# Summed-value and attention projections as three passes of split parts instead of full f32, with the weights split in the stream and at its end

## The chip, the cores and the metric

One core of one Trainium2 chip. The metric is the device time of one execution in microseconds (us), the median of several runs. Engines are TensorE (PE; its weight loads are PEld), VectorE (DVE), ScalarE (ACT), GpSimd (POOL) and SyncE (SP), which issues nearly all loads.

## The reference

One perceiver-like block on x (256 x 512) with a context of 25,088 rows of 512:

```python
x = x + xattn(layernorm(x), ctx)     # sigmoid(q k^T / sqrt(128)) @ (ctx Wv^T + bv), no softmax
x = x + attn(layernorm(x))           # 16 heads of 32, latent k/v of 128, rotary part of 32, causal
x = x + ffn(layernorm(x))            # top-1 of 8 experts: relu(g)^2 * u, masked by the one-hot, @ wd
```

In the cross attention q = Wq x + bq and k = Wk ctx + bk. All is float32.

## The kernel before

**Split operands.** A large product of two f32 matrices is made from three matmuls of float32r operands: each operand is split into a high part (a ScalarE copy to float32r) and a low part (a VectorE subtraction), and high x high, high x low and low x high add up in PSUM. The context, the sigmoid weights, the keys and the expert weights go this way. Other products are full f32 matmuls, each of which the profile shows as two records.

**The stream.** The context comes in 49 blocks of 512 rows, once transposed (`rawt`) and once as it is (`rawn`). For block b the loop at L364 queues scores(b), weights(b) (sigmoid, split), keys(b+1), the splits of the blocks ahead, and values(b), which adds sigmoid^T ctx for both halves of 128 queries into banks 4 and 5. Wv is not applied per context row: it is applied once to the sum. One spare load goes out per block: first the list `late` (L349: wv, latent and rotary weights, gate, tables, bv), then in odd blocks from 15 the expert weights: `up_load` (L354) brings half a megabyte into the staging tile `wst`, and `up_split` (L358) splits it two blocks later. Each tensor of `ups` (L351) has one load and one split; there are eight. At blocks NB-3 and NB-2 come the loads of wq, wo (`DWO`, L387) and the first two parts of wd, into places that the stream has left.

**The end of the stream.** The last blocks are written out by hand (L390 to L402) so that the first half (r = 0) of the sum is done before the second. Then, for a half r: `sum_out` (L422) copies the sum to `y_s`, which is `h_s`; four transposes; `sum_turned` (L425) evicts them on ScalarE to `yT`, which is `hT`; `project_v` (L428) multiplies by wv in full f32: 4 matmuls of 128x512. The bias part, bv times the row sums of the sigmoid, is added to x by two VectorE operations (L466). `norm_stats` (L437) adds the projection to x and computes the statistics, with the square root on ScalarE (L442), and `norm_rows` (L444) normalizes. The second half's values matmuls (L469) lie between the two projections. `latents` (L492) and `query` (L536) follow.

**The attention.** Six units of heads are pipelined by hand (from L676): scores, maxima, exponentials (ScalarE), transposes on TensorE, evictions of them (`a_evac`, L613, on the engine that is named), the product with v (`a_pv`, L621). `a_sums` (L635) makes reciprocals of the sums and spreads them per head (`eexp`), `a_spread` (L642) turns them on TensorE, `a_spread_out` (L649) evicts them to `rr`, and `a_norm` (L652) multiplies the result of a half by them into `aT`. `project_o` (L658) multiplies by wo in full f32, 4 matmuls of 128x512 into bank 1. Then come the residual add, the normalization, and the experts (`experts_up` L761, `down` L793), whose input is split by `norm_parts` (L738). wd is split there by `down_part` (L807).

Each engine executes its queue in the order of the `put` calls, and waits on a semaphore ahead of an instruction where a mark is listed:

```python
XM = [project_v(0, 2, [YT[0], LATE, ZF[last]])]                      # L463
DONE.append(values(last, (1, 2, 3), (1,), sig="av1"))                # L469
X1[0], RS[0] = norm_stats(0, 2, [XM[0], XB])                         # L471
XM.append(project_v(1, 3, [YT[1]]))                                  # L481
XO = [project_o(0, 1, [])]                                           # L720
X2[0], RS[0] = norm_stats(0, 1, [XO[0]])                             # L725
XO.append(project_o(1, 1, [X2[0]]))                                  # L823
```

Of the kernel before, what the change touches and what calls it, by code (L numbers as in the profile page):

```python
# [13 lines left out]
P = 128  # L14
# [44 lines left out]
def program(nc, x, ctxn, ctxt, wkt, wqt, wvt, bqk, bv, kvd, kup, vup, wq, qrope, krope, wo, gate, wg, wu, wd,  # L59
# [3 lines left out]
    with ExitStack() as ctx:  # L63
# [3 lines left out]
        def sb(name, shape, dt=F32):  # L67
            return ctx.enter_context(nc.sbuf_tensor(name, shape, dt))

        ps = [ctx.enter_context(nc.psum_tensor(f"ps{i}", [P, 1024], F32)) for i in range(4)]  # L70

# [6 lines left out]
        x_s = sb("x_s", [P, 2, D])  # L78
        h_s = sb("h_s", [P, 2, D])
        hT = sb("hT", [P, 4, T])  # L80
        st = sb("st", [P, 64])
        sq = sb("sq", [1, 8])
        zacc = sb("zacc", [P, 1024])
        zcol = sb("zcol", [P, 2])
        zsum = sb("zsum", [P, T])
        wz = sb("wz", [P, 512], BF16)
        one_s = sb("one_s", [P, 1])
        wv_s = sb("wv_s", [P, 4, D])
        bv_s = sb("bv_s", [P, D])
# [40 lines left out]
        zl = [sm(f"zl{i}", [P, 1024], F32R) for i in range(2)]  # L130
        wst = sm("wst", [P, 1024])
        stream.close()
# [5 lines left out]
        hTl = sb("hTl", [P, 4, T], F32R)  # L138
        wo_s = sb("wo_s", [P, 4, D])
        wds = [sb(f"wds{i}", [P, 1024]) for i in range(2)]  # L140
        aT = sb("aT", [P, 4, T])
        eexp = sb("eexp", [P, 16, 32])
        rr = sb("rr", [P, D])
        wdh = sb("wdh", [P, 8, D], F32R)
# [11 lines left out]
        ka = sa("ka", [P, 8, T])  # L156
        w_s = [sa(f"w{i}", [P, 512]) for i in range(4)]
        rtx = ExitStack()
# [51 lines left out]
        def split_n(b, k, later=False):  # L210
# [11 lines left out]
            return low if later else low()  # L222

        WZ = put("gpsimd", lambda e: e.memset(wz[:], 0.0), (), "wz")
        for k in range(14):
# [120 lines left out]
        for k in range(2):  # L346
            split_t(1, k)()

        late = [(wv_s[:], wvt), (kvd_s[:], kvd), (qr_s[:], qrope), (kr_s[:], krope), (kup_s[:], kup),  # L349
                (vup_s[:], vup), (gate_s[:], gate), (cs_s[:], cossin), (mk_s[:], mask), (io_s[:], iota), (bv_s[:], bv)]  # L350
        ups = [(w, h, l, c) for w, h, l in ((wg, wgh, wgl), (wu, wuh, wul)) for c in range(4)]  # L351
        UP, DUP = [], []

        def up_load(i):  # L354
            w, h, l, c = ups[i]
            DUP.append(dma("sync", wst[:], w[:, c].rearrange("p a b -> p (a b)"), "dup", UP[-1:]))

        def up_split(i):  # L358
            w, h, l, c = ups[i]
            hi, lo = (t[:, c].rearrange("p a b -> p (a b)") for t in (h, l))  # L360
            m = put("scalar", lambda e: e.activation(hi, wst[:], ACT.Copy), DUP[-1:], "uph")
            UP.append(put("vector", lambda e: e.tensor_tensor(lo, wst[:], hi, ALU.subtract), [m], "upl"))

# [42 lines left out]
        def half(r):  # L406
            return slice(r * P, r * P + P)
# [17 lines left out]
        def sum_turned(r, bk, mark):  # L425
            return put("scalar", lambda e: e.activation(yT[:, :, half(r)], chunks(bk), ACT.Copy), [mark], "yt_e")

        def project_v(r, bk, wait):  # L428
            for c in range(4):
                m = put("tensor", lambda e, c=c: e.matmul(bank(bk), yT[:, c, half(r)], wv_s[:, c, :], start=(c == 0),  # L430
                                                          stop=(c == 3)), wait, "xp" if c == 3 else None)
            return m

        def col(r, k, n=1):
# [25 lines left out]
        for r in range(2):  # L460
            m = put("tensor", lambda e, r=r: e.matmul(bank(0)[:, r:r + 1], zsum[:, half(r)], one_s[:],
                                                      start=True, stop=True), [ZS, ONE, KPL[last]], "zs1" if r else None)
        XM = [project_v(0, 2, [YT[0], LATE, ZF[last]])]  # L463
        ZR = put("vector", lambda e: e.tensor_copy(zcol[:], bank(0)[:, 0:2]), [m], "zr")
        for r in range(2):
            XB = put("vector", lambda e, r=r: e.scalar_tensor_tensor(  # L466
                out=x_s[:, r, :], in0=bv_s[:], scalar=zcol[:, r:r + 1], in1=x_s[:, r, :], op0=ALU.mult, op1=ALU.add),
                [ZR, LATE], "xb")
        DONE.append(values(last, (1, 2, 3), (1,), sig="av1"))  # L469
        X1, RS = [None, None], [None, None]  # L470
# [9 lines left out]
        HT = [put("vector", lambda e: e.tensor_scalar(hT[:, :, half(0)], chunks(0), 2.0, None, ALU.mult), [n], "lne_v")]  # L480
        XM.append(project_v(1, 3, [YT[1]]))  # L481

# [9 lines left out]
        def latents(r, b_c, b_q, b_k, b_v, wait):  # L492
            n = half(r)
            m = project(bank(b_c)[:, 0:P], lambda c: kvd_s[:, c, :], n, [HT[r], *wait], "ck")
            CKV[r] = put("scalar", lambda e: e.activation(ckv[:, n], bank(b_c)[:, 0:P], ACT.Copy), [m], "ckv")
            QR[r] = project(bank(b_q)[:, 0:P], lambda c: qr_s[:, c, :], n, [X1[r], YT[1]], "qr")
            KR[r] = put("tensor", lambda e: e.matmul(bank(b_c)[:, 0:P], kr_s[:], ckv[:, n], start=True, stop=True),
                        [CKV[r]], "kr")
            for t in range(4):
                KT[r] = put("tensor", lambda e, t=t: e.matmul(bank(b_k)[:, P * t:P * t + P], kup_s[:, P * t:P * t + P],  # L500
                                                              ckv[:, n], start=(t == 0), stop=(t == 3)), [X1[r]],
                            "k" if t == 3 else None)
            VT[r] = put("tensor", lambda e: e.matmul(bank(b_v), ckv[:, n], vup_s[:], start=True, stop=True), [], "v")
# [131 lines left out]
        def a_sums(qt):  # L635
            m = put("vector", lambda e: e.reciprocal(einv[:, qt, :], esum[:, qt, :]),
                    [EX[p, u] for p in range(NU) if units[p][0] == qt for u in range(2)], "rc")
            return put("vector", lambda e: e.tensor_copy(
                eexp[:], einv[:, qt, :].rearrange("p (h o) -> p h o", o=1).to_broadcast([P, 16, 32])),
                [m] + ([RR[0]] if qt else []), "rc")  # L640
# [8 lines left out]
        def a_spread_out(qt, bk, mark):  # L649
            RR[qt] = put("scalar", lambda e: e.activation(rr[:], bank(bk), ACT.Copy), [mark] + ([AE[0]] if qt else []), "rr_s")  # L650

        def a_norm(qt):  # L652
            AE[qt] = put("vector", lambda e: e.tensor_tensor(
                aT[:, :, half(qt)], bank(1 + qt).rearrange("p (t n) -> p t n", t=4),
                rr[:].rearrange("p (t n) -> p t n", t=4), ALU.mult),
                [RR[qt]] + [PV[p] for p in range(NU) if units[p][0] == qt], "ae")

        def project_o(r, bk, wait):  # L658
            for t in range(4):
                m = put("tensor", lambda e, t=t: e.matmul(bank(bk), aT[:, t, half(r)], wo_s[:, t, :], start=(t == 0),  # L660
                                                          stop=(t == 3)), [AE[r], DWO, *wait], "wo" if t == 3 else None)
            return m
# [48 lines left out]
        a_scores(5)  # L711
        a_norm(0)
        maxima(5)
        turns(4)
        a_evac(4, 0, "scalar")
        a_evac(4, 1, "vector")
        exps(5)
        a_pv(3)
        table(ACT.Sqrt)
        XO = [project_o(0, 1, [])]  # L720
        X2 = [None, None]
        f = a_spread(1, 4, [a_sums(1), EX[4, 0]])
        a_spread_out(1, 4, f)
        turns(5)
        X2[0], RS[0] = norm_stats(0, 1, [XO[0]])  # L725
        a_evac(5, 0, "scalar")
# [3 lines left out]
        a_pv(5)  # L730
        a_norm(1)

# [28 lines left out]
        def experts_up(r, k, j, wait):  # L761
            wh, wl = ((wgh, wgl), (wuh, wul))[j]
            n = 0
            for c in range(4):
                for w, h in ((wh, hTh), (wh, hTl), (wl, hTh)):
                    n += 1
                    GU[r, k, j] = put("tensor", lambda e, w=w, h=h, c=c, n=n: e.matmul(  # L767
                        bank(UB[k][j]), h[:, c, half(r)], w[:, c, 4 * k:4 * k + 4, :].rearrange("p a b -> p (a b)"),
                        start=(n == 1), stop=(n == 12)), [HP[r][0], UP[-1], *wait], "gu" if n == 12 else None)
# [37 lines left out]
        def down_part(k):  # L807
            n = slice(2 * k, 2 * k + 2)
            h_, l_ = (t[:, n].rearrange("p a b -> p (a b)") for t in (wdh, wdl))
            m = put("scalar", lambda e: e.activation(h_, wds[k % 2][:], ACT.Copy), [DWD[k], DONE[1]], "wdh")  # L810
            WDP.append(put("vector", lambda e: e.tensor_tensor(l_, wds[k % 2][:], h_, ALU.subtract), [m], "wdl"))
# [9 lines left out]

        m = norm_turn(0, 6, [EX[4, 1]])
        XO.append(project_o(1, 1, [X2[0]]))  # L823
        norm_parts(0, 6, m)
# [123 lines left out]
```

How the kernel before makes its waits and increments, by code:

```python
    def play(self, eng, e):  # L49
        for item in self.lists[eng]:
            if item[0] == "wait":
                e.wait_ge(item[1], item[2])
            else:
                ins = item[1](e)
                if item[2] is not None:
                    ins.then_inc(item[2], item[3])
```

## Time and profile before

| | |
|---|---|
| median of 3 runs | 585.0 us (584.59 to 585.08) |
| profiled execution | 584.42 us, span 582.6 us |
| busy: PE, DVE, ACT | 571.4, 448.5, 392.8 us |
| chain that ended last | PE 93%, DVE 3%, ACT 2% |
| granted clock of TensorE | 1.0 |

The span reaches from the first to the last instruction in the profile; the rest of the execution's time lies around it. Busy times overlap between engines. The chain is followed back from the last instruction, at each step to what released it, or to the one before it on its engine.

### The profile page before, as it was taken

What the parts mean: (1) busy time and instruction counts of PE and PEld (TensorE: products, weight loads), DVE (VectorE), ACT (ScalarE), POOL (GpSimd) and SP (SyncE); (2) the same over time, 40 slices, a digit from 0 to 9 for tenths busy, and PEclk for the clock granted to TensorE, in tenths of its full rate; (3) what the DMA queues carried; (4) which work ended last, traced back from release to release, by engine and by line L of the source; (5) the groups of instructions that cost most, each with busy time, mean ns of one, the idle gap of its engine ahead of it and who ended that gap; (6) DMA issues with size and microseconds to landing.
All of it is one profiled execution on the core that took longest, in us unless ns stands there. A gap on an engine that the chain in (4) does not pass through costs nothing.

```text
span 582.6 us, 7921 instructions
## 1 busy us (share of the span) xinstructions
PE 571.4 (98%) x2966; PEld 472.8 (81%) x2966; DVE 448.5 (77%) x499; ACT 392.8 (67%) x529; POOL 1.7 (0%) x7
## 2 busy tenths in 40 slices
PE   7899999999999999999999999999999999999998
PEld 4788888888888888888888888888888885766787
DVE  5887878787878798889788978787878775786642
ACT  5776677776767787868786767777776772586321
POOL 1000000000000000000000000000000000000000
DMA  8678877777777877787778676767676752000200
GB/s 278 206 242 271 257 245 243 221 224 224 228 229 243 260 246 233 244 258 251 240 237 259 216 228 208 231 210 228 208 244 193 246 174 118 1 2 2 72 1 36
DMA packets 33094, 115.87 MB, mean 199 GB/s; under 512 B 4065, under 2 KB 4769, under 8 KB 32673
## 3 DMA queue, kind: packets, MB, share of 16 engines
q1 hardware_dynamic: 32480, 114.79, 62.4%
q10 hardware_dynamic: 576, 0.59, 0.3%
q8 instruction: 23, 0.38, 0.3%
q14 instruction: 15, 0.11, 0.1%
HBM read 114.84 MB, written 0.52 MB: 198 GB/s over the span
## 4 chain that ended last, share of the span: by engine, by line
PE 93%; DVE 3%; ACT 2%; DMA 1%; issue 1%; DVEq 0%; SPq 0%
PE ps L327 45%; PE ps L275 22%; PE ps L292 12%; PE ps L767 4%; PE ps L799 2%; PE ps L486 2%; PE ps L660 1%; PE ps L430 1%; ACT w L601 1%; DMA rawt<-in_ctxt 1%; PE ps L579 1%; DMA x_s<-in_x 1%; PE ps L608 1%; DVE zl L307 0%; DVE tl L204 0%
## 5 line engine op out<-in xcount | busy, mean ns | idle before, releaser
L327 PE MATMUL ps<-nh,zl 128*128 128x512 f32 x392 | 144.8, 390 | 0.4 <-DVE zl L307 0.3
L327 PE MATMUL ps<-nh,zh 128*128 128x512 f32 x392 | 144.9, 390 | 0.0
L327 PE MATMUL ps<-nl,zh 128*128 128x512 f32 x392 | 144.4, 389 | 0.0
L307 DVE TENSOR_TENSOR zl<-zf,zh 128x1024 fp32r<-128x1024 f32 x49 | 60.1, 1226 | 83.4 <-ACT zh L306 83.4
L216 DVE TENSOR_TENSOR nl<-rawn,nh 128x1024 fp32r<-128x1024 f32 x98 | 116.7, 1221 | 4.2 <-ACT nh L213 2.5
L204 DVE TENSOR_TENSOR tl<-rawt,th 128x1024 fp32r<-128x1024 f32 x98 | 115.6, 1218 | 2.2 <-ACT th L199 2.1
L213 ACT ACTIVATE nh<-rawn 128x1024 fp32r<-128x1024 f32 x98 | 101.6, 1056 | 14.1 <-DMA rawn<-in_ctxn 13.5
L199 ACT ACTIVATE th<-rawt 128x1024 fp32r<-128x1024 f32 x98 | 98.6, 1053 | 5.4 <-DMA rawt<-in_ctxt 5.4
L302 ACT ACTIVATE zf<-ps 128x512 f32<-128x512 f32 x98 | 58.2, 597 | 56.7 <-PE ps L292 51.1
L327 PEld LDWEIGHTS ps<-nh,zl 128*128 128x128 f32 x392 | 73.4, 188 | 17.0 <-DVE zl L307 1.7
L327 PEld LDWEIGHTS ps<-nh,zh 128*128 128x128 f32 x392 | 73.4, 188 | 15.6 <-issue 0.2
L327 PEld LDWEIGHTS ps<-nl,zh 128*128 128x128 f32 x392 | 73.6, 188 | 15.3
L280 ACT ACTIVATE kph<-ps,bqk_s 128x512 fp32r<-128x512 f32 x49 | 33.8, 689 | 49.4 <-PE ps L275 49.4
L310 DVE TENSOR_TENSOR zacc<-zacc,zf 128x1024 f32<-128x1024 f32 x49 | 59.8, 1221 | 0.0
L292 PE MATMUL ps<-qph,kph 128*128 128x256 f32 x196 | 55.3, 282 | 1.2 <-DVE qpl L343 1.2
L292 PE MATMUL ps<-qph,kpl 128*128 128x256 f32 x196 | 55.5, 283 | 0.0
L292 PE MATMUL ps<-qpl,kph 128*128 128x256 f32 x196 | 55.4, 283 | 0.0
L275 PE MATMUL ps<-th,wkh 128*128 128x512 f32 x196 | 54.1, 396 | 0.7 <-ACT th L199 0.7
L306 ACT ACTIVATE zh<-zf 128x1024 fp32r<-128x1024 f32 x49 | 52.1, 1063 | 1.6
L275 PE MATMUL ps<-th,wkl 128*128 128x512 f32 x196 | 52.6, 390 | 0.0
L275 PE MATMUL ps<-tl,wkh 128*128 128x512 f32 x196 | 52.4, 389 | 0.0
L275 PEld LDWEIGHTS ps<-th,wkl 128*128 128x128 f32 x196 | 36.8, 188 | 8.3
(154 smaller groups left out, 575.0 us busy)
## 6 DMA issues: line engine op xcount, KB each, us to landing
rawt<-in_ctxt SPq DMA_DIRECT2D x98, 512.0 KB, 4.7
rawn<-in_ctxn SPq DMA_DIRECT2D x98, 512.0 KB, 6.4
wst<-in_wg SPq DMA_DIRECT2D x4, 512.0 KB, 7.3
wst<-in_wu SPq DMA_DIRECT2D x4, 512.0 KB, 7.4
wds<-in_wd SPq DMA_DIRECT2D x4, 512.0 KB, 4.8
wv_s<-in_wvt SPq DMA_DIRECT2D x1, 1024.0 KB, 9.9
wq_s<-in_wq SPq DMA_DIRECT2D x1, 1024.0 KB, 7.1
wo_s<-in_wo SPq DMA_DIRECT2D x1, 1024.0 KB, 4.7
```

Source lines behind the costliest of these rows:

```text
L199: Th[b, k] = put("scalar", lambda e: e.activation(th[:, n], rawt[:, n], ACT.Copy), [t_ld[b, k]] + before, "th")
L204: Tl[b, k] = put("vector", lambda e: e.tensor_tensor(tl[:, n], rawt[:, n], th[:, n], ALU.subtract), [t_ld[b, k], Th[b, k]], "tl")
L213: Nh[b, k] = put("scalar", lambda e: e.activation(nh[s_][:, n], rawn[:, n], ACT.Copy), [n_ld[b, k]] + av, "nh")
L216: Nl[b, k] = put("vector", lambda e: e.tensor_tensor(nl[s_][:, n], rawn[:, n], nh[s_][:, n], ALU.subtract), [n_ld[b, k], Nh[b, k]] + av, "nl")
L275: KP[b] = put("tensor", lambda e, w=w, t=t, c=c, i=i: e.matmul(bank(b % 2), w[:, c * P:(c + 1) * P], t[:, c * 512:(c + 1) * 512], start=(i ...
L280: KPH[b] = put("scalar", lambda e: e.activation(kph[:], bank(b % 2), ACT.Identity, bias=bqk_s[:, 1:2]), [KP[b], DBK] + ([S[b - 1]] if b el ...
L292: m = put("tensor", lambda e, o=o, js=js, k=k, w=w, i=i: e.matmul(o, k[:, js], w[:], start=(i == 0), stop=(i == 2)), wait, "s" if (i == 2 ...
L302: m = put("scalar", lambda e, g=g, gs=gs: e.activation(zf[:, gs], bank(2 + g), ACT.Sigmoid, scale=SC), [S[b, g]] + ([ZL[b - 1], ZA[b - 1]] ...
L306: ZH[b] = put("scalar", lambda e: e.activation(zh[b % 2][:], zf[:], ACT.Copy), [ZF[b]] + av, "zh")
L307: ZL[b] = put("vector", lambda e: e.tensor_tensor(zl[b % 2][:], zf[:], zh[b % 2][:], ALU.subtract), [ZH[b]] + av, "zl")
L310: ZA[b] = put("vector", lambda e: e.tensor_tensor(zacc[:], zacc[:], zf[:], ALU.add), [ZF[b], Z0] + ([ZA[b - 1]] if b else []), "za")
L327: AV[b] = put("tensor", lambda e, z=z, n=n, i=i, j=j, r=r: e.matmul(bank(4 + r), z[:, j * T + r * P:j * T + r * P + P], n[:, j * D:(j + 1) ...
```

## The change

`project_v` and `project_o` become three passes of float32r parts, 12 matmuls for 4. Each needs its two operands in high and low parts:

- wv leaves `late`. It is loaded in two pieces as the first two entries of `ups`, now ten, and split like the expert weights. The staging tile is `h_s`.
- wo is split by `split_o` in two pieces, the high ones on ScalarE right after the first `project_v` is queued, the low ones on VectorE ahead of the first residual add and after the first `hT` eviction.
- `sum_turned` evicts the high part on ScalarE and the low part on VectorE.
- `a_norm` makes the high part first; the returned function makes the full product and the low part. For the first half it is queued after the last `turns(4)` and its first eviction.
- the first `project_o` goes to bank 6, and the second norm's waits follow.
- the three passes of `experts_up` are reordered, and wd's split waits for the second `project_o`.
- tiles share places: yTh with hT, yTl with eexp, rr and zacc, w_s with wvh, aT and the parts of a with wvl, wol with wo_s, wst with h_s.

```diff
-        late = [(wv_s[:], wvt), (kvd_s[:], kvd), (qr_s[:], qrope), ...
+        late = [(kvd_s[:], kvd), (qr_s[:], qrope), ...
+        ups = [tuple(flat(t[:, 2 * k:2 * k + 2]) for t in (wvt, wvh, wvl)) for k in range(2)]
+        ups += [tuple(flat(t[:, c]) for t in m) for m in ((wg, wgh, wgl), (wu, wuh, wul)) for c in range(4)]
...
         def up_load(i):
-            w, h, l, c = ups[i]
-            DUP.append(dma("sync", wst[:], w[:, c].rearrange("p a b -> p (a b)"), "dup", UP[-1:]))
+            DUP.append(dma("sync", wst, ups[i][0], "dup", UP[-1:]))
...
         def sum_turned(r, bk, mark):
-            return put("scalar", lambda e: e.activation(yT[:, :, half(r)], chunks(bk), ACT.Copy), [mark], "yt_e")
+            hi = put("scalar", lambda e: e.activation(yTh[:, :, half(r)], chunks(bk), ACT.Copy), [mark], "yt_e")
+            lo = put("vector", lambda e: e.tensor_tensor(yTl[:, :, half(r)], chunks(bk), yTh[:, :, half(r)], ALU.subtract),
+                     [hi, ZS], "yt_l")
+            return hi, lo
...
         def project_v(r, bk, wait):
-            for c in range(4):
-                m = put("tensor", lambda e, c=c: e.matmul(bank(bk), yT[:, c, half(r)], wv_s[:, c, :], start=(c == 0),
-                                                          stop=(c == 3)), wait, "xp" if c == 3 else None)
+            hi, lo = YT[r]
+            for i, (t, w, mark) in enumerate(((yTh, wvh, hi), (yTh, wvl, hi), (yTl, wvh, lo))):
+                for c in range(4):
+                    m = put("tensor", lambda e, t=t, w=w, c=c, i=i: e.matmul(
+                        bank(bk), t[:, c, half(r)], w[:, c, :], start=(i == 0 and c == 0), stop=(i == 2 and c == 3)),
+                        [mark, UP[1], *wait], "xp" if (i, c) == (2, 3) else None)
             return m
+
+        def split_o(k):
+            n = slice(2 * k, 2 * k + 2)
+            hi = put("scalar", lambda e: e.activation(flat(woh[:, n]), flat(wo_s[:, n]), ACT.Copy), [DWO], "woh")
+            return lambda: put("vector", lambda e: e.tensor_tensor(flat(wol[:, n]), flat(wo_s[:, n]), flat(woh[:, n]),
+                                                                   ALU.subtract), [hi], "wol")
...
-        XM = [project_v(0, 2, [YT[0], LATE, ZF[last]])]
+        XM = [project_v(0, 2, [ZF[last]])]
+        low_o = [split_o(k) for k in range(2)]
         ZR = put("vector", lambda e: e.tensor_copy(zcol[:], bank(0)[:, 0:2]), [m], "zr")
...
+        low_o[0]()
         DONE.append(values(last, (1, 2, 3), (1,), sig="av1"))
...
         HT = [put("vector", lambda e: e.tensor_scalar(hT[:, :, half(0)], chunks(0), 2.0, None, ALU.mult), [n], "lne_v")]
-        XM.append(project_v(1, 3, [YT[1]]))
+        WOL = low_o[1]()
+        XM.append(project_v(1, 3, []))
...
         def a_norm(qt):
...
+            AH[qt] = put("vector", lambda e: e.tensor_tensor(aTh[:, :, n], src, r4, ALU.mult), done, "ah")
+
+            def rest():
+                AE[qt] = put("vector", lambda e: e.tensor_tensor(aT[:, :, n], src, r4, ALU.mult), [], "ae")
+                AL[qt] = put("vector", lambda e: e.tensor_tensor(aTl[:, :, n], aT[:, :, n], aTh[:, :, n], ALU.subtract),
+                             [AE[qt]], "al")
+
+            return rest
 
         def project_o(r, bk, wait):
...
+            for i, (t, w, mark) in enumerate(((aTh, woh, AH[r]), (aTh, wol, AH[r]), (aTl, woh, AL[r]))):
+                for c in range(4):
+                    m = put("tensor", lambda e, t=t, w=w, c=c, i=i: e.matmul(
+                        bank(bk), t[:, c, n], w[:, c, :], start=(i == 0 and c == 0), stop=(i == 2 and c == 3)),
+                        [mark, WOL, *wait],
+                        "wo" if (i, c) == (2, 3) else None)
...
-        a_norm(0)
+        low_a = a_norm(0)
         maxima(5)
         turns(4)
         a_evac(4, 0, "scalar")
+        low_a()
         a_evac(4, 1, "vector")
         exps(5)
         a_pv(3)
         table(ACT.Sqrt)
-        XO = [project_o(0, 1, [])]
+        XO = [project_o(0, 6, [EX[4, 1]])]
...
-        X2[0], RS[0] = norm_stats(0, 1, [XO[0]])
+        X2[0], RS[0] = norm_stats(0, 6, [XO[0]])
...
-        a_norm(1)
+        a_norm(1)()
...
-                for w, h in ((wh, hTh), (wh, hTl), (wl, hTh)):
+                for w, h in ((wh, hTh), (wl, hTh), (wh, hTl)):
...
-            m = put("scalar", lambda e: e.activation(h_, wds[k % 2][:], ACT.Copy), [DWD[k], DONE[1]], "wdh")
+            m = put("scalar", lambda e: e.activation(h_, wds[k % 2][:], ACT.Copy), [DWD[k], XO[1]], "wdh")
...
-        m = norm_turn(0, 6, [EX[4, 1]])
-        XO.append(project_o(1, 1, [X2[0]]))
+        m = norm_turn(0, 6, [X2[0]])
+        XO.append(project_o(1, 1, [AE[0]]))
```

## Rows read from the trace of the kernel before

**Rows 1.** The page: the span, and busy time of each engine

```profile
span 582.6 us, 7921 instructions
...
PE 571.4 (98%) x2966; PEld 472.8 (81%) x2966; DVE 448.5 (77%) x499; ACT 392.8 (67%) x529; POOL 1.7 (0%) x7
```

**Rows 2.** Chain of waits, 180 to 220 us: start, duration, engine, tile, line

```profile
184.97 5.44 PE ps L327 x24
190.41 1.43 PE ps L292 x12
191.84 2.75 PE ps L275 x12
```

**Rows 3.** Windows of two blocks: length, busy (instructions) per engine, PE clock, DMA

```profile
240.00:259.20 19.20, 19.20 (x97) 16.38 (x96) 15.94 (x16) 14.74 (x17) 0.00 (x0) 1.00 0.82 245
...
343.20:362.40 19.20, 19.20 (x97) 16.34 (x97) 15.08 (x15) 13.63 (x17) 0.00 (x0) 1.00 0.73 219
```

**Rows 4.** Chain of waits, 480 to 545 us, around the summed values

```profile
485.28 3.56 PE ps L430 x8
488.86 0.70 DVE x_s L438
...
492.86 3.59 PE ps L430 x8
```

**Rows 5.** Chain of waits, 490 us to the end

```profile
530.39 3.65 PE ps L660 x8
...
534.06 0.70 DVE x_s L438
...
538.79 3.70 PE ps L660 x8
542.49 5.61 PE ps L767 x24
...
574.30 5.76 PE ps L799 x48
```

**Rows 6.** The page's costly groups: busy, mean ns of one, idle before

```profile
L327 PE MATMUL ps<-nh,zh 128*128 128x512 f32 x392 | 144.9, 390 | 0.0
```

**Rows 7.** Tiles wst and wkl: ns min/median/max, first and last start

```profile
L361 ACT ACTIVATE wuh<-wst x4: 1043/1044/1047, 266.8 to 324.1; 128x1024 fp32r<-128x1024 f32 x4
L362 DVE TENSOR_TENSOR wul<-wst,wuh x4: 1221/1223/1224, 268.4 to 326.1; 128x1024 fp32r<-128x1024 f32 x4
...
L256 DVE TENSOR_TENSOR wkl<-wk_s,wkh x1: 682/682/682, 8.4 to 8.4; 128x512 fp32r<-128x512 f32 x1
```

**Rows 8.** Timeline of ScalarE, 480 to 496 us

```profile
484.28 0.60 ACT L426 ACTIVATE hT<-ps 128x512 f32<-128x512 f32 x1 [0.74 <-PE ps L411]
490.71 0.20 ACT L442 ACTIVATE st<-st 128x1 f32<-128x1 f32 x1 [5.84 <-DVE st L441]
490.92 0.66 ACT L472 ACTIVATE h_s<-ps 128x256 f32<-128x256 f32 x2
```

**Rows 9.** Timeline of VectorE, 484 to 496 us

```profile
485.31 0.16 DVE L464 COPY zcol<-ps 128x2 f32<-128x2 f32 x1 [1.45 <-PE ps L461]
485.51 1.41 DVE L466 SCALAR_TENSOR_TENSOR x_s<-bv_s,zcol,x_s 128x512 f32<-128x512 f32 x2
```

**Rows 10.** Tiles wo_s and wv_s: issue of the load and its landing

```profile
L47 SPq DMA_DIRECT2D wo_s<-in_wo x1: 328/328/328, 478.2 to 478.2; - x1
...
DMA to landing us min/median/max: 4.7/4.7/4.7
...
DMA to landing us min/median/max: 9.9/9.9/9.9
```

**Rows 11.** Timeline of VectorE, 518 to 536 us

```profile
530.63 0.68 DVE L619 COPY wT<-ps 128x512 f32<-128x512 f32 x1
532.02 0.25 DVE L636 RECIPROCAL einv<-esum 128x16 f32<-128x16 f32 x1 [0.71 <-ACT w L601]
532.31 0.43 DVE L638 COPY eexp<-einv 128x512 f32<-128x512 f32 x1
```

More of the change, by code:

```diff
@@ L68, in sb, with several, once @@
             return ctx.enter_context(nc.sbuf_tensor(name, shape, dt))
+        def several(name, n, shape, dt=F32):
+            with ExitStack() as group:
+                return [group.enter_context(nc.sbuf_tensor(f"{name}{i}", shape, dt)) for i in range(n)]
+        def once(name, shape, dt=F32):
+            with nc.sbuf_tensor(name, shape, dt) as t:
+                return t
         ps = [ctx.enter_context(nc.psum_tensor(f"ps{i}", [P, 1024], F32)) for i in range(4)]
@@ L79, in program @@
         h_s = sb("h_s", [P, 2, D])
+        yTh = once("yTh", [P, 4, T], F32R)
         hT = sb("hT", [P, 4, T])
@@ L82, in program @@
         sq = sb("sq", [1, 8])
+        yTl = once("yTl", [P, 4, T], F32R)
+        eexp, rr = (t[:] for t in several("er", 2, [P, D]))
+        eexp = eexp.rearrange("p (h o) -> p h o", o=32)
         zacc = sb("zacc", [P, 1024])
         zcol = sb("zcol", [P, 2])
+        wz = once("wz", [P, 512], BF16)
         zsum = sb("zsum", [P, T])
-        wz = sb("wz", [P, 512], BF16)
         one_s = sb("one_s", [P, 1])
-        wv_s = sb("wv_s", [P, 4, D])
+        w_s = several("w", 4, [P, 512])
+        wvh = sb("wvh", [P, 4, D], F32R)
+        aT, _ = several("aT", 2, [P, 4, T])
+        aTl, aTh = several("aTs", 2, [P, 4, T], F32R)
+        wvl = sb("wvl", [P, 4, D], F32R)
         bv_s = sb("bv_s", [P, D])
@@ L130, in program @@
         zl = [sm(f"zl{i}", [P, 1024], F32R) for i in range(2)]
-        wst = sm("wst", [P, 1024])
         stream.close()
@@ L138, in program @@
         hTl = sb("hTl", [P, 4, T], F32R)
-        wo_s = sb("wo_s", [P, 4, D])
+        wo_s = once("wo_s", [P, 4, D])
+        wol = sb("wol", [P, 4, D], F32R)
+        woh = sb("woh", [P, 4, D], F32R)
         wds = [sb(f"wds{i}", [P, 1024]) for i in range(2)]
-        aT = sb("aT", [P, 4, T])
-        eexp = sb("eexp", [P, 16, 32])
-        rr = sb("rr", [P, D])
         wdh = sb("wdh", [P, 8, D], F32R)
@@ L156, in program @@
         ka = sa("ka", [P, 8, T])
-        w_s = [sa(f"w{i}", [P, 512]) for i in range(4)]
         rtx = ExitStack()
@@ L222, in split_n @@
             return low if later else low()
+        wst = h_s[:].rearrange("p a b -> p (a b)")
         WZ = put("gpsimd", lambda e: e.memset(wz[:], 0.0), (), "wz")
@@ L347, in program, with flat @@
             split_t(1, k)()
-        late = [(wv_s[:], wvt), (kvd_s[:], kvd), (qr_s[:], qrope), (kr_s[:], krope), (kup_s[:], kup),
+        late = [(kvd_s[:], kvd), (qr_s[:], qrope), (kr_s[:], krope), (kup_s[:], kup),
                 (vup_s[:], vup), (gate_s[:], gate), (cs_s[:], cossin), (mk_s[:], mask), (io_s[:], iota), (bv_s[:], bv)]
-        ups = [(w, h, l, c) for w, h, l in ((wg, wgh, wgl), (wu, wuh, wul)) for c in range(4)]
+        def flat(t):
+            return t.rearrange("p a b -> p (a b)")
+        ups = [tuple(flat(t[:, 2 * k:2 * k + 2]) for t in (wvt, wvh, wvl)) for k in range(2)]
+        ups += [tuple(flat(t[:, c]) for t in m) for m in ((wg, wgh, wgl), (wu, wuh, wul)) for c in range(4)]
         UP, DUP = [], []
         def up_load(i):
-            w, h, l, c = ups[i]
-            DUP.append(dma("sync", wst[:], w[:, c].rearrange("p a b -> p (a b)"), "dup", UP[-1:]))
+            DUP.append(dma("sync", wst, ups[i][0], "dup", UP[-1:]))
         def up_split(i):
[L359 to L362, printed above, removed]
+            _, hi, lo = ups[i]
+            m = put("scalar", lambda e: e.activation(hi, wst, ACT.Copy), DUP[-1:], "uph")
+            UP.append(put("vector", lambda e: e.tensor_tensor(lo, wst, hi, ALU.subtract), [m], "upl"))
         for b in range(NB):
@@ L495, in latents @@
             CKV[r] = put("scalar", lambda e: e.activation(ckv[:, n], bank(b_c)[:, 0:P], ACT.Copy), [m], "ckv")
-            QR[r] = project(bank(b_q)[:, 0:P], lambda c: qr_s[:, c, :], n, [X1[r], YT[1]], "qr")
+            QR[r] = project(bank(b_q)[:, 0:P], lambda c: qr_s[:, c, :], n, [X1[r], YT[1][0]], "qr")
             KR[r] = put("tensor", lambda e: e.matmul(bank(b_c)[:, 0:P], kr_s[:], ckv[:, n], start=True, stop=True),
@@ L638, in a_sums @@
             return put("vector", lambda e: e.tensor_copy(
-                eexp[:], einv[:, qt, :].rearrange("p (h o) -> p h o", o=1).to_broadcast([P, 16, 32])),
+                eexp, einv[:, qt, :].rearrange("p (h o) -> p h o", o=1).to_broadcast([P, 16, 32])),
                 [m] + ([RR[0]] if qt else []), "rc")
@@ L649, in a_spread_out @@
         def a_spread_out(qt, bk, mark):
-            RR[qt] = put("scalar", lambda e: e.activation(rr[:], bank(bk), ACT.Copy), [mark] + ([AE[0]] if qt else []), "rr_s")
+            RR[qt] = put("scalar", lambda e: e.activation(rr, bank(bk), ACT.Copy), [mark] + ([AE[0]] if qt else []), "rr_s")
+        AH, AL = {}, {}
         def a_norm(qt):
[L653 to L656, printed above, removed]
-        def project_o(r, bk, wait):
-            for t in range(4):
-                m = put("tensor", lambda e, t=t: e.matmul(bank(bk), aT[:, t, half(r)], wo_s[:, t, :], start=(t == 0),
-                                                          stop=(t == 3)), [AE[r], DWO, *wait], "wo" if t == 3 else None)
+            src = bank(1 + qt).rearrange("p (t n) -> p t n", t=4)
+            r4 = rr[:].rearrange("p (t n) -> p t n", t=4)
+            n = half(qt)
+            done = [RR[qt]] + [PV[p] for p in range(NU) if units[p][0] == qt]
+            AH[qt] = put("vector", lambda e: e.tensor_tensor(aTh[:, :, n], src, r4, ALU.mult), done, "ah")
[4 more added lines that the diff above has]
+            return rest
+        def project_o(r, bk, wait):
+            n = half(r)
+            for i, (t, w, mark) in enumerate(((aTh, woh, AH[r]), (aTh, wol, AH[r]), (aTl, woh, AL[r]))):
[4 more added lines that the diff above has]
+                        "wo" if (i, c) == (2, 3) else None)
             return m
```

## Prediction

> **What bounds the kernel now.** I read the page first. TensorE (PE) is busy 571 of 582.6 us [rows 1], so only what shortens its queue, or a wait of that queue, can move the end. The chain of waits in a stretch of the stream shows the period of one block of context: values 5.44, scores 1.43, key projection 2.75, that is 9.62 us of TensorE back to back, with nobody else in it [rows 2]. The windows say how much room the others have there: in 19.2 us TensorE is busy 19.20, VectorE 15.94 and ScalarE 14.74 where two expert weights are split, 15.08 and 13.63 where none is, with the same 97 matmuls, and the granted clock is 1.00, the higher level of 2.4 GHz [rows 3]. So the stream is TensorE's alone. After it, from about 480 us, the chain goes back and forth: each projection that the change touches stands on it (3.56 and 3.59 us for the summed values, 3.65 and 3.70 us for the attention), followed by VectorE's residual add and statistics [rows 4, 5]. From 542.49 us TensorE is on the chain without a break to 580.05 [rows 5], so whatever is gained up to the fourth projection should reach the end whole.
>
> **Price of a projection.** Before: four full f32 matmuls, 8 records, 3.56 to 3.70 us [rows 4, 5]. After: 12 matmuls of reduced-precision operands, same 128x512 size. Their nearest row is the expert matmuls in the same part of the kernel, 24 in 5.61 us, 0.234 each [rows 5]; in the stream 24 take 5.44, 0.227 each [rows 2]. One such record lasts 0.39 against a spacing of 0.234 [rows 6], so a last one adds 0.16 for whoever waits for it. 12 x 0.234 + 0.16 = 2.97 us against 3.56, 3.59 and 3.65: a gain of 0.59, 0.62 and 0.68. I take 0.64 for each of the four. The lower bound is 0.59. For the upper one, suppose that a reduced-precision pass takes no longer than a quarter of a full f32 matmul: (3.65 - 0.16) / 16 = 0.218, so 12 x 0.218 + 0.16 = 2.78, and a gain of 0.87.
>
> The rows put the gain at 0.64, since the 12 passes are spaced 0.234 apart and the quarter of a full f32 matmul is only 0.218. The Trainium skill has one spacing for both: "FP8 and Floating Point Precision", section TensorE Precision Notes, counts full f32 as four passes through the array, and "TensorE: Matmul & The Clock Gate", section Back-to-back issue gap, gives a pass N/2.4 + 2.5 ns, about 216 ns for 512 columns; 16 against 12 such passes would save 0.86. The trace agrees for full f32 and not for the reduced operands, and the measured spacing decides; equal spacing is a rival below.
>
> **Splits in the stream.** wv (1 MB) is no longer one late load but two staged ones, so the queue of expert weights has ten entries for eight: two more ScalarE copies of 1.04 and VectorE subtractions of 1.22 us [rows 7], in blocks of their own. They are covered by VectorE's 3.3 us and ScalarE's 4.5 us of room in two blocks [rows 3]; uncovered they would cost 2.3 each. The bytes on SP's queue are the same, and each staged load waits for a split that is already done in the blocks that do this now, where TensorE doesn't stop. Cost 0. The staging buffer now shares its place with h_s, idle in the stream: 0.
>
> **First projection of the summed values.** The high part replaces an eviction of the same size, 484.28 to 484.88 [rows 8]. The low part is new on VectorE: 0.69 (an operation from PSUM, as the residual add in [rows 4]), to 485.61; TensorE needs it after 8 of 12 matmuls, near 487.0, so it costs nothing there. But it stands ahead of the copy of the row sums and of the two bias additions (0.16 and 1.41 us [rows 9]), which end near 487.3, and behind these the change puts the first half of wo's low part, 1.22 [rows 7], to 488.5. TensorE is done with the projection at 488.83 - 0.64 = 488.2. So the residual add starts at 488.5, not 488.2, where it was at 488.86 [rows 4]: **0.34** of the 0.64 arrive. wo's two high parts (2 x 1.04) fill a ScalarE that waits 5.8 us there [rows 8]; they need wo_s, issued at 478.2 and landed 4.7 us later, at 482.9 [rows 10], two us early.
>
> The 0.34 go on: statistics, square root at 490.37, then the evictions of the second half's sum, which stand behind that root on ScalarE at 490.92 [rows 8], then transposes. The values matmuls they also need end earlier by 0.64.
>
> **Second projection of the summed values.** Its low part follows the row normalization on VectorE and is ready 0.7 after its high part, against 1.87 us (8 matmuls) of cover. hT's eviction and wo's second low part (1.22) come next and end near 495.0; the residual add waits for TensorE until 495.5. All covered: **0.64**. The latents and the attention up to 530 us are bound to this end on both engines, so everything there moves by 0.98.
>
> **First attention projection** (times as before, without that 0.98). The high part takes the place of aT's multiply. The full product and the low part stand between the last maxima and the copy of a transposed tile that ran at 530.63 [rows 11]. They cost 0.69 + 0.68 (the second is the one subtraction of this size within SBUF, [rows 7]) with two handovers: 1.4. The copy then ends at 532.7, the reciprocal and its spread (from 532.02 to 532.74 before [rows 11]) at 533.5. TensorE starts the projection at 530.39 as before, runs 8 matmuls to 532.26, when the low part (ready near 532.05) is just there, and ends at 530.39 + 2.97 = 533.4. So the residual add moves from 534.06 [rows 5] to about 533.55: **0.50**, bounds 0.3 and 0.64. Moving it to bank 6 costs nothing: that score tile has been read by then. The exponentials on ScalarE don't wait for the added work.
>
> **Second attention projection.** The chain comes through the last evictions and the product with v ahead of it, all 0.50 earlier, to the high part. The full and low products end 1.45 after it, against 1.87 of cover, and the next stage's low part (0.69) behind them still ends some 0.9 before the experts need it. **0.64**. The swapped order of the expert passes changes no count: all of them wait for the low part anyway. The later wait of wd's split costs 0: ScalarE reaches it after the square root, which comes after that projection.
>
> Sum: 0.34 + 0.64 + 0.50 + 0.64 = 2.12. The profiled execution took 584.42 us (span 582.6 and 1.8 around it), 0.6 under the median of 585.0; 584.42 - 2.12 = 582.3, and against the median **582.9 us**.
>
> **Rivals.**
> - *VectorE's queue eats more.* Both first halves end in VectorE, not in TensorE, by 0.3 and 0.1. If its added pieces with their handovers take 0.35 to 0.5 longer in each place, the first halves bring nothing and 2 x 0.64 = 1.3 is left: 583.7. For it: the order of its queue. Against: all pieces have rows.
> - *TensorE gives the full four.* If VectorE overlaps its operations a little more, 4 x 0.64 = 2.56: 582.4.
> - *Equal spacing.* If the new passes run at the 0.218 of full f32, 0.87 comes in each of the two that TensorE alone bounds and 0.84 together where VectorE bounds: 2.58, 582.4; with VectorE out of the way too, 4 x 0.87 = 3.5, 581.5. The spacings of [rows 2, 5] speak against it. This is the Trainium skill's rule named above.
> - *No gain.* The latents' stage or attention is bound by something that doesn't move with the projections (a queue on ScalarE, say). Then at most the last 0.64 to 1.1 stay: 584 to 584.4. The chain shows no such wait in the places that I followed.
> - *Slower: wo_s is late.* wo's high part stands on ScalarE and its low part on VectorE ahead of the residual add. If the load lands at L, that add cannot start before L + 1.06 + 1.26. At 488.2 or later, 10.0 us after issue instead of 4.7, the whole gain of 2.1 is gone, and from 11.2 us on the kernel is slower by over 1.2: 586.2 and more. For it: the other 1 MB load, wv_s, took 9.9 in the full stream [rows 10]. Against: this one runs when the stream's loads are over.
> - *The passes are no cheaper*, because the split operands are treated as full f32: 12 at 0.86 would be 10 us each. The key projections of the stream, split in the same way, exclude it.
>
> **How the numbers follow.** Forecast 0.67; VectorE's queue 0.13; full four 0.07; equal spacing 0.04; no gain 0.04; wo_s late 0.04; passes no cheaper, or what I haven't seen, 0.01. A measurement of this kernel can tell about 0.2%, 1.2 us, from no change, that is 583.8. Faster takes the forecast, the two larger gains and 0.08 of VectorE's case: 0.86. Same takes the rest of that case and no gain: 0.09. Slower: 0.05. The range runs from 581.6, nearly the whole of equal spacing, to 584.0, just past the case of VectorE's queue.
>
> **What would show it.** In the changed profile: the block period still 9.62; each projection 12 matmuls at about 0.234; the first residual add released by wo's low part on VectorE and not by TensorE, 0.3 earlier than now; TensorE's first latents 1.0 earlier; at the first attention projection the residual add 1.5 earlier; the experts 2.1 earlier (from 542.49 to 540.4) and from there the same 37.6 us. It is wrong if the period grows, if TensorE idles over 0.2 us between the eighth and the ninth matmul of a projection, or if the stretch from 496.5 to 530.4 gets longer.

## The result and the profile after

The change makes the kernel faster, by 0.4%: 582.60 us median of 7 runs (581.88 to 583.38) against 584.52 (584.30 to 585.08) in the same comparison, ratio 0.9964, 95% interval 0.9952 to 0.9975. Two later comparisons of the same kernel gave 582.08 against 584.68 (0.9957, 0.9945 to 0.9969) and 581.97 against 584.63 (0.9958, 0.9945 to 0.9972). Over all 18 runs of it the median is 582.2, some 2.4 us under before. The forecast was 2.1, from 585.0 to 582.9.

The profiled execution took 581.88 us, 2.54 less than the one of before. Its page, span and busy times (compare [rows 1]):

```profile
span 580.1 us, 7972 instructions
...
PE 570.3 (98%) x2982; PEld 475.8 (82%) x2982; DVE 456.7 (79%) x509; ACT 398.3 (69%) x533; POOL 1.7 (0%) x7
```

TensorE has 16 records more (four for each projection) and is busy 1.1 us less, VectorE 8.2 us more. TensorE's busy time in the first 50 us differs from profile to profile and is 1.2 us longer in this one (45.94 for 44.76); from 50 us on it is 2.3 us shorter. The chain of waits in the stream (start, duration, engine, tile, line) shows the block period unchanged, 5.44 + 1.43 + 2.75 = 9.62, as in [rows 2]:

```profile
50.18 5.44 PE ps L341 x24
55.62 1.43 PE ps L306 x12
57.05 2.75 PE ps L289 x12
```

The chain after the stream, the lines that answer to [rows 4, 5]:

```profile
485.33 2.92 PE ps L452 x12
488.25 0.02 issue
488.28 0.70 DVE x_s L467
...
492.28 2.97 PE ps L452 x12
...
529.18 2.98 PE ps L704 x12
...
536.93 3.02 PE ps L704 x12
539.95 5.60 PE ps L814 x24
...
571.75 5.76 PE ps L846 x48
```

The four projections took 3.56, 3.59, 3.65 and 3.70 us and take 2.92, 2.97, 2.98 and 3.02. Each is shorter by 0.62 to 0.68, and the starts behind them move by steps of that size: the first residual add from 488.86 to 488.28, the second projection of the attention from 538.79 to 536.93, the experts from 542.49 to 539.95.

One more thing is in this profile. The chain near 476 us is not TensorE's, as it was before, but goes through a load:

```profile
470.52 5.85 DMA rawn<-in_ctxn
476.38 0.02 issue
476.40 0.04 ACT nh L226
476.44 0.92 issue
477.36 1.08 ACT zf L316 x2
```

The last half block of `rawn` landed late, ScalarE's split of it (nh) held the sigmoid (zf) behind it in its queue, and TensorE waited for the sigmoid weights. To keep such noise of a single execution out, I cut every profile at two marks: the end of the last block's score matmuls, and the start of the first `project_v`. The stretch behind the second mark is the same within 0.06 us in the three profiles of the change, and so is the one ahead of the first mark: from the values matmuls of the fourth block to the last scores all profiles take 426.0 us. What else differs between the profiled spans lies in the first 50 us: these values start between 49.66 and 50.51.

Worked out from the timelines, us after the start of the first `project_v`:

| kernel | last scores to that start | 1st, 2nd add (values) | 1st, 2nd add (attention) | end |
|---|---|---|---|---|
| before | 7.43 | 3.72, 11.35 | 48.92, 57.38 | 97.46 |
| changed, first profile | 7.55 | 3.09, 10.10 | 47.01, 54.80 | 94.91 |
| changed, second | 7.40 | 3.08, 10.08 | 46.98, 54.78 | 94.92 |
| changed, third | 7.43 | 3.07, 10.08 | 47.04, 54.84 | 94.97 |
| v_only | 7.43 | 3.08, 10.09 | 47.65, 56.12 | 96.18 |
| o_only | 7.43 | 3.72, 11.35 | 48.26, 56.06 | 96.21 |
| low_o_behind | 7.84 | 3.08, 10.69 | 47.61, 55.41 | 95.51 |
| low_o_both | 7.95 | 4.17, 11.05 | 48.04, 55.83 | 95.91 |
| low_a_behind | 7.76 | 3.07, 10.08 | 47.52, 55.31 | 95.40 |
| four_passes | 7.57 | 3.99, 11.91 | 49.74, 58.46 | 98.56 |
| wq_late | 7.41 | 3.08, 10.10 | 47.01, 54.79 | 94.92 |
| wq_late_2 | 7.43 | 3.08, 10.09 | 47.00, 54.79 | 94.86 |
| before_wq_late | 7.41 | 3.71, 11.35 | 48.91, 57.38 | 97.47 |

Before against the second profile of the change: 0.64, then 1.27, 1.94 and 2.60 at the four adds, 2.54 at the end. So the steps are 0.64, 0.63, 0.67 and 0.66, all four in full; 0.06 of them is lost again behind the last add.

### The profile page after: what moved, and what is told of

Read it like the earlier page. It is cut to its first block, busy times and chain, and to the rows that moved or that the text cites. A ratio compares the mean times of both kernels' runs of the same rounds, so it can differ in the third digit from the quotient of the medians.

```text
span 580.1 us, 7972 instructions
## 1 busy us (share of the span) xinstructions
PE 570.3 (98%) x2982; PEld 475.8 (82%) x2982; DVE 456.7 (79%) x509; ACT 398.3 (69%) x533; POOL 1.7 (0%) x7
## 4 chain that ended last, share of the span: by engine, by line
PE 91%; DVE 3%; ACT 3%; DMA 2%; issue 1%; DVEq 0%; SPq 0%
PE ps L341 44%; PE ps L289 22%; PE ps L306 11%; PE ps L814 4%; PE ps L846 2%; PE ps L518 2%; PE ps L704 1%; PE ps L452 1%; DMA rawn<-in_ctxn 1%; ACT w L633 1%; DMA rawt<-in_ctxt 1%; PE ps L611 1%; PE ps L640 1%; DMA x_s<-in_x 1%; ACT th L212 1%
```

## The experiments

**The change again** (r_after, then r_after_2). No edit.

> The changed kernel once more, as it is. In its first profile the gain was 2.54 us (span 582.6 to 580.1) where the medians differed by 1.92 (584.52 to 582.60), and its runs spread over 1.5 us where those of before spread over 0.8. Theory A, a late load at the end of the stream (the last half of rawn shares the queues with wq_s and held ScalarE's nh to 476.40, 0.36 ahead of nothing that TensorE could cover): the median stays near 582.6, the spread stays over 1 us, and a profile of a slower execution loses its time between 470 and 481 us. Rival B, chance of the first seven runs: median 582.0 and a spread like before's.

Median 582.08 (581.69 to 582.49, 6 runs). The first comparison's 1.9 us was on the low side. The spread was 0.8, not over 1, and this profile, in which no late load reaches TensorE (7.40), shows nothing lost: the repeat speaks for chance as to how large the gain is. On the load it decides nothing.

> The changed kernel a third time, as the partner of the next run. Theory A (the late half of rawn costs 0 to 0.5 us between the last scores and the first projection, from execution to execution): median near 582.2, the profile shows 7.4 to 7.95 us from the last scores to the start of the first projection. The stretch from that start to the end is 94.9 in any case.

581.97 (581.70 to 583.10, 5 runs), 7.43 and 94.97. The fixed stretch came as expected; the median lies 0.2 under the expected one.

**Each half alone.** v_only puts `project_o`, `a_norm` and their waits back as they were and drops `split_o`; o_only does the same with `sum_turned`, `project_v` and wv's load:

```diff
# v_only
-        low_o = [split_o(k) for k in range(2)]
...
-        low_o[0]()
...
-        WOL = low_o[1]()
...
-        XO = [project_o(0, 6, [EX[4, 1]])]
+        XO = [project_o(0, 1, [])]
...
# o_only
-        late = [(kvd_s[:], kvd), ...
+        late = [(wv_s[:], wvt), (kvd_s[:], kvd), ...
...
-        ups = [tuple(flat(t[:, 2 * k:2 * k + 2]) for t in (wvt, wvh, wvl)) for k in range(2)]
...
-        XM = [project_v(0, 2, [ZF[last]])]
+        XM = [project_v(0, 2, [YT[0], LATE, ZF[last]])]
```

> Three passes for the summed values alone, the attention projections full f32 as before. By the sum of steps with what the first profile shows: 0.66 + 0.63 = 1.3 us under before. Rival (the v half brings only 1.0, the 0.3 being lost to wo's low part on VectorE, which is absent here): 1.3 here and a smaller difference between this kernel and the full change than 1.3. Places of tiles are those of the changed kernel, so if they or the two more stream splits cost something, this kernel gains less than 1.0.

> Three passes for the attention alone, wv in one late load and full f32 as before. By the steps: 0.65 + 0.68 = 1.3 us under before, and together with the other half it adds up to the full change (2.6 in a profile, 1.9 in medians). If VectorE's added pieces hold the attention's residual add, 0.9 to 1.1 only. If the stream's two more splits cost time in the full change, the two halves add up to more than the full change.

By the profiles each half brings 1.28 and 1.25 us (97.46 less 96.18 and 96.21), together 2.53, the whole. The first add of v_only comes at 3.08, exactly where the full change has it with wo's low part ahead of it on VectorE: that piece took nothing. By its rival 0.3 of the first add would have come back here and some 1.0 would be left between v_only and the full change; it is 96.18 - 94.92 = 1.26, so the rival is out.

The medians are coarser: 583.95 (12 runs, ratio 0.9991, 0.9981 to 1.0001) and 583.28 (12 runs, 0.9979, 0.9969 to 0.9990), gains of 0.7 and 1.4. v_only by itself can't be told from no change; its single runs lie between 582.5 and 585.3. Its 0.7 is also less than the 1.0 that I had named as the sign that the new places or the stream's splits cost something. Its profile doesn't bear that out, with the same 426.0 us up to the last scores (49.66 to 475.66). Part of the difference lies outside the span, where three of its twelve executions have 2.5 to 3.1 us instead of some 1.8 (the medians of the spans are 0.95 and 1.45 under those of before). Where its slower executions lose the rest no trace shows: the profiled one is the second fastest of the twelve.

The chain of waits in v_only has one kind of projection next to the other:

```profile
484.66 2.91 PE ps L452 x12
...
491.60 2.97 PE ps L452 x12
...
528.51 3.64 PE ps L683 x8
...
536.90 3.70 PE ps L683 x8
```

**Where wo's low part stands.**

```diff
# low_o_behind
-        low_o[0]()
         DONE.append(values(last, (1, 2, 3), (1,), sig="av1"))
...
         X1[0], RS[0] = norm_stats(0, 2, [XM[0], XB])
+        low_o[0]()
# low_o_both
         low_o[0]()
+        WOL = low_o[1]()
...
-        WOL = low_o[1]()
         XM.append(project_v(1, 3, []))
```

> The changed kernel with the first half of wo's low part queued on VectorE behind the statistics of the first residual add instead of ahead of it. In the profile of the change that low part ends at 488.31 and TensorE's projection at 488.25, so both release the add. Theory (the forecast's 0.30 held by VectorE has shrunk to under 0.1, since independent VectorE operations overlap): the add starts within 0.1 us of where it does, at 488.2, and the time from the last scores to the end stays at 102.3 within 0.1. Rival (VectorE's queue holds it): the add starts 0.3 earlier. It must not get slower than by 0.1, unless the low part then delays the evictions behind it.

> The changed kernel with both halves of wo's low part ahead of the first residual add: 1.22 us more on VectorE there, 1.22 less after hT's eviction. Theory: there is no room left at this place, so the add starts 1.1 to 1.2 us later (489.4), the evictions behind the square root and the second projection with it, and the time from the last scores to the end grows by 1.1 to 1.2; median 1.0 to 1.3 above the changed kernel. Rival (the place had 0.5 or more of room, TensorE being the one that releases): 0.5 to 0.7 only.

Behind the statistics, the add starts at 3.08 as before the move, so nothing had held it: the rival is out. But the kernel gets 0.6 us longer (95.51). That I had expected to be under 0.1, with a condition that named the wrong place: it isn't the evictions behind it, it is the row normalization. VectorE's timeline of low_o_behind:

```profile
489.94 0.16 DVE L470 TENSOR_SCALAR st<-st 128x1 f32<-128x1 f32 x1
490.01 1.22 DVE L460 TENSOR_TENSOR wol<-wo_s,woh 128x1024 fp32r<-128x1024 f32 x1
491.14 0.16 DVE L476 RECIPROCAL st<-st 128x1 f32<-128x1 f32 x1
```

The reciprocal that needs the square root stands behind 1.22 us of subtraction; it used to follow the statistics by 0.42 (489.95 to 490.37). The delay is 491.14 - 490.36 = 0.78, of which 0.61 reach the second add. Median 582.51 (6 runs).

With both halves ahead, the add comes at 4.17 for 3.08:

```profile
487.79 2.35 DVE L460 TENSOR_TENSOR wol<-wo_s,woh 128x1024 fp32r<-128x1024 f32 x2
490.06 0.68 DVE L467 TENSOR_TENSOR x_s<-ps,x_s 128x512 f32<-128x512 f32 x1
```

1.09 later for 1.13 us of added work, and the end 0.99 later (95.91; median 583.21, 10 runs, 1.0 over the 582.2 of the change): the theory, a little under its 1.1 to 1.2 at both places. So the room at this place is under 0.1 us: the one low part fits exactly, and the next is paid nearly in full. Both results together say that VectorE and TensorE come to the add within some hundredths of each other, with TensorE deciding.

**The low part of the attention.**

```diff
-        low_a()
         a_evac(4, 1, "vector")
+        low_a()
```

> The changed kernel with the full product and the low part of the first half of the attention queued behind the eviction of the transposed tile instead of ahead of it. The low part is then ready 0.6 us later, at 531.45 instead of 530.83, while TensorE has 8 of 12 matmuls until about 531.0. Theory: TensorE waits 0.4 us between the eighth and the ninth matmul, and the residual add comes 0.4 later, end of the kernel +0.4. Rival (the low part had more cover): no change within 0.1 and the spread of the reciprocals as before.

TensorE's timeline of low_a_behind shows the wait:

```profile
529.41 1.20 PE L704 MATMUL ps<-woh,aTs 128*128 128x512 f32 x4
530.45 1.08 PE L704 MATMUL ps<-wol,aTs 128*128 128x512 f32 x4
531.79 1.19 PE L704 MATMUL ps<-woh,aTs 128*128 128x512 f32 x4 [0.25 <-DVE aTs L695]
```

The third four start 1.34 after the second four, where they start 0.92 after them in the change:

```profile
530.16 1.08 PE L704 MATMUL ps<-wol,aTs 128*128 128x512 f32 x4
531.08 1.08 PE L704 MATMUL ps<-woh,aTs 128*128 128x512 f32 x4
```

That is 0.42 lost. The four behind the wait also last 1.19 for 1.08, so the add comes 0.54 later (47.52 for 46.98), and the end 0.48 (95.40 for 94.92). The order in the change is the right one of the two. Its low part is ready at 530.83, 0.25 ahead of the ninth matmul: eight matmuls cover the two VectorE operations with that much to spare. Median 582.52 (12 runs).

**A fourth pass.** This adds low x low, so the projections compute slightly more than in the change.

```diff
-            for i, (t, w, mark) in enumerate(((yTh, wvh, hi), (yTh, wvl, hi), (yTl, wvh, lo))):
+            for i, (t, w, mark) in enumerate(((yTh, wvh, hi), (yTh, wvl, hi), (yTl, wvh, lo), (yTl, wvl, lo))):
...
# the same in project_o
```

> All four projections with a fourth pass, low x low, 16 matmuls for 12: this measures a pass of reduced operands against the quarter of a full f32 matmul that it replaces. By the spacing of the rows (0.233 against 0.218): +0.93 us for each projection that TensorE bounds, +3.6 in all, so 1.0 us slower than the kernel with full f32 projections, whose four passes are the same arithmetic. By equal spacing: +0.87 each, +3.5 at most and the same time as before the split, apart from VectorE's queue. From the last scores to the end: 105.9 by the first, 105.3 or less by the second, against 104.9 before the change.

The chain of waits of four_passes:

```profile
485.18 3.83 PE ps L452 x16
...
493.04 3.87 PE ps L452 x16
...
530.85 3.90 PE ps L704 x16
```

98.56 to the end against 94.92: 3.64 for 16 added matmuls, 0.228 each. Against full f32 (3.56, 3.59, 3.65) the four passes cost 0.25 to 0.28 more per projection, 1.10 in all, and the kernel is slower than before by as much: 585.54 (10 runs) against 584.50, ratio 1.0020 (1.0010 to 1.0029). A pass of the split operands is dearer than a quarter of a full f32 matmul, 0.228 to 0.234 against 0.218; the gain comes from the pass left out, not from the format. From the last scores to the end it takes 106.1, over both expected numbers (105.9 and 105.3); a late load is in it, and with the usual 7.43 it is 98.56 + 7.43 = 106.0, at the first theory's.

Why a pass of split operands is dearer is not shown. One difference stands in TensorE's weight loads, of which every record has one. In the first projection they read, before and after:

```profile
486.08 0.19 PEld L430 LDWEIGHTS ps<-wv_s,hT 128*128 128x128 f32 x1 [0.24 <-issue]
485.99 0.89 PEld L452 LDWEIGHTS ps<-wvl,yTh 128*128 128x128 f32 x4
```

Full f32 has eight loads of 0.19 us, 0.43 apart; the three passes have twelve, 0.23 apart, with next to nothing between them. No run separates the loads from the matmuls.

**The late load.** All of wq_late is that wq_s, first read at 504 us, is loaded last instead of right behind the last half of `rawn`, which is what ScalarE waits for:

```diff
-                if b == NB - 3:
-                    DWQ2 = dma("sync", wq_s[:], wq, "dwq2", t_rd[NB - 1, 0] + t_rd[NB - 1, 1])
...
                     DWD = [dma("sync", wds[k][:], ...
                                [KP[NB - 1]]) for k in range(2)]
+                    DWQ2 = dma("sync", wq_s[:], wq, "dwq2", t_rd[NB - 1, 0] + t_rd[NB - 1, 1])
```

> The changed kernel with the load of wq_s issued last, behind those of wo_s and wds, one block later. Theory A: rawn's last half lands up to 1 us earlier, ScalarE's nh no longer delays the last sigmoid, the median falls by 0.3 to 0.9 us to 581.7 to 582.3 and the spread shrinks under 0.8. Rival B: no change of median or spread within 0.2 us, the wait of nh stays. wq_s is needed only near 503 us, so its lateness costs nothing.

> The changed kernel with the load of wq_s issued last, again. Theory A: 0.3 to 0.6 us under the changed kernel in the median (it was 581.51 against 582.08), 7.41 us from the last scores to the first projection, rawn's last half landed within 5.3 us of its issue. Rival B: the two medians within 0.2, the earlier difference was chance.

> The kernel before with the load of wq_s issued last. Theory A is not about the change, so it should help here too if the load is late here as often: 0 to 0.5 us under before. If before already has 7.43 us from the last scores to the first projection in nearly every execution, no difference.

ScalarE's timeline in low_o_behind, where the load came late, has the second nh 1.51 us idle before it:

```profile
476.39 1.06 ACT L226 ACTIVATE nh<-rawn 128x1024 fp32r<-128x1024 f32 x1 [1.51 <-DMA rawn<-in_ctxn]
477.36 1.07 ACT L316 ACTIVATE zf<-ps 128x512 f32<-128x512 f32 x2
```

and in wq_late_2 the wait is gone: both run in one go, and the sigmoid waits for TensorE alone:

```profile
474.19 2.00 ACT L226 ACTIVATE nh<-rawn 128x1024 fp32r<-128x1024 f32 x2
477.04 1.32 ACT L316 ACTIVATE zf<-ps 128x512 f32<-128x512 f32 x2 [0.85 <-PE ps L306]
```

The slower of the last two halves of `rawn` lands 3.9 to 4.7 us after its issue in the three profiles with the late wq, and 4.9 to 6.3 us in the ten others. The stretch from the last scores to the first projection is 7.41, 7.43 and 7.41 us in the three, and 7.40 to 7.95 in the others. The medians are 581.51 (6 runs) and 581.89 (5), against 582.08 and 581.97 of the change in the same comparisons: lower by 0.57 and by 0.08. The ratios to before, 0.9948 (0.9935 to 0.9961) and 0.9952 (0.9938 to 0.9965), are the lowest of all kernels here, but their intervals overlap the change's. On the kernel before it gives 584.37 (11 runs) against 584.63, ratio 0.9993 (0.9984 to 1.0002). That the load's lateness costs up to 0.5 us in an execution is shown. That moving wq_s gains in the median is not: the first run's 0.57 was within theory A, the second's 0.08 is what rival B said. Nor is the late load what spreads the executions. With it gone the spread was 1.3 in wq_late, where I had expected under 0.8, and single runs of one kernel differ by 0.8 to 3.3 us in these comparisons.

## Why the prediction was right, point by point

- **Bound and cover.** The stream's two more splits cost nothing: from the values of the fourth block to the last scores both kernels take 426 us (50.28 to 476.28, and 50.18 to 476.2), and so does o_only, which hasn't the splits (49.93 to 475.93). The stretch from 496.5 to 530.4, which was not to get longer, takes 33.93 us in both (496.46 to 530.39, 495.25 to 529.18), and the one from the experts to the end of the chain's last matmuls 37.56 in both.
- **Price of a projection, 0.64.** Measured 0.64, 0.63, 0.67, 0.66. The expert matmuls were the right row; equal spacing is refuted by four_passes, and with it the figure of 0.86 that the Trainium skill ("FP8 and Floating Point Precision", section TensorE Precision Notes, with "TensorE: Matmul & The Clock Gate", section Back-to-back issue gap) would give with the spacing that it states for an isolated matmul. The page's count of four passes for full f32 fits the trace, where a quarter of such a matmul takes 0.218 us, near its 0.216; its one spacing for both doesn't.
- **First projection of the summed values, forecast 0.34, measured 0.64.** This is the step that failed: VectorE was to release this add, and TensorE did. I put wo's low part end to end with the operations before it and let it finish at 488.5. VectorE's timeline of the change:

```profile
484.96 0.69 DVE L444 TENSOR_TENSOR yTl<-ps,yTh 128x512 fp32r<-128x512 f32 x1 [1.03 <-ACT yTh L443]
485.57 0.15 DVE L494 COPY zcol<-ps 128x2 f32<-128x2 f32 x1
485.76 1.42 DVE L496 SCALAR_TENSOR_TENSOR x_s<-bv_s,zcol,x_s 128x512 f32<-128x512 f32 x2
487.09 1.22 DVE L460 TENSOR_TENSOR wol<-wo_s,woh 128x1024 fp32r<-128x1024 f32 x1
488.28 0.69 DVE L467 TENSOR_TENSOR x_s<-ps,x_s 128x512 f32<-128x512 f32 x1
```

Where an operation doesn't need the result of the one ahead of it, the two overlap by 0.03 to 0.09 us: the low part of y lasts until 485.65 and the copy behind it starts at 485.57; the bias additions last until 487.18 and wo's low part starts at 487.09. It ends at 488.31, 0.2 earlier than I had it, and TensorE at 488.25. The trace of before showed this overlap too, and I didn't use it:

```profile
528.43 0.69 DVE L653 TENSOR_TENSOR aT<-ps,rr 128x512 f32<-128x512 f32 x1 [1.20 <-ACT rr L650]
529.04 0.68 DVE L592 TENSOR_REDUCE sm_s<-ps 128x2 f32<-128x512 f32 x1
```

- **Second projection of the values, forecast 0.64, measured 0.63.** All the cover that was named held.
- **First attention projection, forecast 0.50, measured 0.67.** The same error: the spread of the reciprocals ends at 532.06, 0.1 before TensorE's projection (531.08 + 1.08 = 532.16), where I had it 0.1 behind. VectorE's timeline of the change:

```profile
531.63 0.43 DVE L670 COPY er<-einv 128x512 f32<-128x512 f32 x1
532.20 0.69 DVE L467 TENSOR_TENSOR x_s<-ps,x_s 128x512 f32<-128x512 f32 x1
```

No idle time stands between the eighth and the ninth matmul, and low_a_behind shows how near that was.
- **Second attention projection, forecast 0.64, measured 0.66.** The three VectorE operations behind it were covered. From the second add to the end it is 40.1 us in both kernels.
- **Sum.** 2.12 was forecast, 2.54 is what the profiles show, so the rival "TensorE gives the full four" (2.56) is what happened in them; I had given it a chance of 0.07. The median of the first comparison gave 1.92, of all runs 2.4. With spreads of 0.8 to 1.5 us among the executions of the changed kernel, the first comparison could have shown either. That its gain came out nearer to the forecast's 2.12 than to the rival's 2.56 was luck: the range held, and the price of a projection was right, but what VectorE was to hold back, 0.44 in the two first projections, it didn't.
- **Slower, by a late wo_s.** It landed 4.8 us after issue; its high part started as soon as ScalarE was free. The load that did come late was another, rawn's, which I hadn't looked at for what it does to a single execution.

## What to carry to other kernels

If three passes of reduced operands replace one full f32 matmul, count the passes: one in four is saved, less 5 to 7% on the others (by this kernel's 0.228 to 0.234 against 0.218), so here a 128x512 projection with four chunks of contraction gains 0.64 us of 3.6, and only if its low parts find VectorE time under the first two passes. The price is the product low x low, which is left out. Put the operands that exist early into the first passes and the one that is made last into the third. Where a filler operation is slipped into an engine's queue, look at what stands behind it: the same 1.22 us were free ahead of an add that waits for a matmul, cost 0.6 behind the statistics, and 1.0 when there were two of them.

## What the runs showed that I had not expected

The passes of split operands are spaced 0.228 to 0.234 us where a quarter of a full f32 matmul takes 0.218, measured in the same place (four passes 3.83 to 3.90, full f32 3.56 to 3.65). And one 1 MB load, issued 0.5 us after the 512 KB that are needed at once, delays these: they land 4.9 to 6.3 us after issue for 3.9 to 4.7, and ScalarE's idle time before nh is 0.3 to 1.6 us in the ten profiles with the old order, 0.2 at most in the three with wq_s last. The time from the last scores to the first projection moved by 0 to 0.5 us with it.
